# A DLRM tower on one core: both gram rounds at the head of each tile's step, the transposes next to the lookups

## The reference

```
e = stack([tbl_f[ids[:, f]] for f in range(26)], axis=1)          # 2048 x 26 x 128
combined = concatenate([dense[:, None, :], e], axis=1)            # 2048 x 27 x 128
interactions = einsum('bnd,bmd->bnm', combined, combined)
z = concatenate([dense, interactions[:, triu_i, triu_j]], axis=1) # 128 + 351
h = concatenate([z, dense], axis=1)                               # 607
h = maximum(h @ W_top1 + b_top1, 0)                               # 512
h = maximum(h @ W_top2 + b_top2, 0)                               # 256
y = h @ W_top3                                                    # 1
```

## Time and profile before

| | us |
|---|---|
| median of 3 timed runs | 425.25 |
| lowest and highest | 422.16, 428.37 |
| span of the profiled execution | 631.9 |
| TensorE matmul busy in it | 404.1 |
| GpSimd busy in it | 281.3 |
| VectorE busy in it | 222.2 |
| ScalarE busy in it | 198.5 |

### The profile page before, as it was taken

One profiled execution on the slowest core, in us unless ns is written; L12 is line 12 of the kernel. 1 busy time (PEld: TensorE's weight loads), 2 busy tenths in 40 slices (PEclk: granted clock), 3 DMA queues, 4 the chain that ended last, 5 costly groups with the idle time before them and its releaser, 6 DMA issues.

```text
span 631.9 us, 14126 instructions
## 1 busy us (share of the span) xinstructions
PE 404.1 (64%) x6097; PEld 357.1 (57%) x6097; DVE 222.2 (35%) x216; ACT 198.5 (31%) x286; POOL 281.3 (45%) x293
## 2 busy tenths in 40 slices
PE   2620774625966487842887568674486946968677
PEld 2610663624856375832777556574475835858566
DVE  4631454514533152412334144140351414534221
ACT  2410223222434142420244214232041421435523
POOL 6777427372535437360272625546046362630000
PEclk9775678777878679875697758896579866879878
DMA  5642102212111122012020121111212012110010
GB/s 133 189 154 55 35 23 57 79 51 78 38 36 38 45 75 56 23 46 75 15 56 22 47 82 35 48 29 47 64 26 56 26 46 77 38 32 32 28 56 1
DMA packets 22371, 33.91 MB, mean 54 GB/s; under 512 B 8300, under 2 KB 15036, under 8 KB 22310
## 3 DMA queue, kind: packets, MB, share of 16 engines
q0 software_dynamic: 9248, 18.93, 11.6%
q1 hardware_dynamic: 13062, 14.04, 6.8%
HBM read 29.30 MB, written 3.68 MB: 52 GB/s over the span
## 4 chain that ended last, share of the span: by engine, by line
PE 53%; issue 24%; another core or an unknown queue 11%; ACT 5%; DMA 3%; DVE 2%; SPq 1%; ACTq 0%; DVEq 0%
PE hot_ps L566 21%; PE gram_ps L590 12%; PE transpose_ps L543 4%; PE mlp_ps L613 4%; PE mlp_ps L603 3%; PE mlp_ps L601 3%; PE mlp_ps L602 3%; DMA embed_t<-table 3%; ACT embed_t L385 2%; PE hot_ids_ps L548 1%; DVE one_hot L460 1%; ACT embed_t L348 1%; ACT hidden_hi L360 1%; DVE table_lo L464 0%
## 5 line engine op out<-in xcount | busy, mean ns | idle before, releaser
L322 POOL DMA_INDIRECT rows<-table,ids_sb x288 | 280.4, 974 | 277.2 <-PE transpose_ps L543 176.5
L566 PE MATMUL hot_ps<-one_hot,table_hi 125*128 125x256 f32 x512 | 170.7, 354 | 71.4 <-ACT embed_t L385 53.5
L460 DVE TENSOR_TENSOR one_hot<-hot_ids_ps,row_numbers_sb 125x1024 fp32r<-125x1024 f32 x128 | 156.2, 1233 | 129.1 <-remote 68.1
L566 PEld LDWEIGHTS hot_ps<-one_hot,table_hi 125*128 125x128 f32 x512 | 122.2, 239 | 79.4 <-issue 38.6
L566 PE MATMUL hot_ps<-one_hot,table_lo 125*128 125x256 f32 x512 | 158.2, 330 | 3.5 <-issue 3.5
L590 PE MATMUL gram_ps<-embed_t 128*27 128x27 f32 x4096 | 79.8, 213 | 118.5 <-issue 113.9
L590 PEld LDWEIGHTS gram_ps<-embed_t 128*27 128x27 f32 x4096 | 63.1, 125 | 137.7 <-issue 133.3
L566 PEld LDWEIGHTS hot_ps<-one_hot,table_lo 125*128 125x128 f32 x512 | 123.2, 241 | 4.3 <-issue 4.3
L348 ACT COPY embed_t<-transpose_ps 128x512 f32<-128x512 f32 (+1 forms) x80 | 92.8, 1160 | 81.0 <-remote 43.0
L446 DVE COPY_PREDICATED units<-late_sb,gram_ps 128x208 f32<-128x208 int32 x32 | 34.8, 1089 | 159.8 <-ACT units L379 159.6
L385 ACT COPY embed_t<-hot_ps 128x256 f32<-128x256 f32 x64 | 44.4, 694 | 81.0 <-PE hot_ps L566 41.5
(11 more groups left out here) (40 smaller groups left out, 242.7 us busy)
## 6 DMA issues: line engine op xcount, KB each, us to landing
rows<-table,ids_sb POOLq DMA_INDIRECT x288
embed_t<-table SPq DMA_DIRECT2D x8, 500.0 KB
bounce<-units SPq DMA_DIRECT2D x8, 448.0 KB, 2.5
scratch<-bounce SPq DMA_DIRECT2D x7, 378.0 KB
rows<-dense SPq DMA_DIRECT2D x16, 64.0 KB
scratch<-w SPq DMA_DIRECT2D x1, 512.0 KB
scratch<-w_units SPq DMA_DIRECT2D x2, 252.0 KB
rows<-bounce SPq DMA_DIRECT2D x1, 378.0 KB
```

The lines of the kernel that those rows point to most:

```text
L322: nc.gpsimd.indirect_dma_start(rows[:, t2, f, :], None, tables[table], bass.IndirectOffsetOnAxis(ids_sb[:, slot, table:table + 1], 0)).the ...
L460: nc.vector.tensor_tensor(one_hot[:, half], ids_over, numbers_over, ALU.is_equal).then_inc(one_hot_ready, 1)
L566: last = nc.tensor.matmul(hot_ps[:, 0:GROUP], table[:, k, step, :], one_hot[:, half, j, :], start=(step == 0 and table is table_hi), stop= ...
```

## The change

In both lists of `STEPS` G1 comes right behind G0, at the head of the step. The five transpose banks follow, each behind one lookup, and the MLP stages come later in the first step (M2 after M1; Q4 ahead of M0) and stay between lookups in the second. Since the last round of a group is now done early in the second step, its pack may reach its landing while the MLP of the group before still uses `scratch`; SP therefore waits, between the store and the landing, for the copy of M6 of the group before (`MLP_USES` is 7). The last group's landing is elsewhere and has no such wait.

```diff
 STEPS = [
-    "B0 G0 H0 H1 Q0 G1 H2 Q1 H3 S0 Q2 H4 Q3 H5 W0 M0 H6 W1 M1 Q4 M2 H7 W2 M3".split(),
-    "G0 H8 M4 H9 Q0 M5 H10 Q1 H11 M6 H12 Q2 H13 W3 Q3 H14 W4 Q4 H15 G1".split(),
+    "B0 G0 G1 H0 Q0 H1 Q1 H2 Q2 H3 Q3 S0 H4 Q4 H5 W0 M0 H6 W1 M1 M2 H7 W2 M3".split(),
+    "G0 G1 H8 Q0 M4 H9 Q1 M5 H10 Q2 H11 Q3 M6 H12 Q4 H13 W3 H14 W4 H15".split(),
 ]
@@
                 sp.dma_start(bounce, units[:, buf].rearrange("p k q -> p (k q)")).then_inc(units_stored, 16)
                 sp.wait_ge(units_stored, 16 * (g + 1))
 
+                if landing is packed_raw:
+                    sp.wait_ge(mlp_copied, MLP_USES * g + 1)
                 by_row = bounce.rearrange("(s n) x -> s (n x)", s=BLOCK)[:, 0:N * UNITS * GROUP_BLOCKS]
```

## The result

The changed kernel takes 457.5 us (455.6 to 458.3, 4 runs), the kernel before 425.2 (422.2 to 428.4, 4 runs): 1.075 times as long, 95% interval 1.070 to 1.081. I forecast 423. (Single executions over 1.5% above the fastest of their kernel stay in the medians given here; the ratios leave them out.)

What follows compares the result with a forecast made beforehand. The prediction took GpSimd's gathers to bound the kernel (407 to 423 us): 10.4 us of new TensorE waits vanish in 48 us of slack, and the earlier pack brings 2, so 425.25 - 2 = 423 us, range 411 to 436.

Steps and rivals of the forecast that it cites:

- The breaks: TensorE's issue waits in the gram rounds, taken as a recording cost: 152 and 70 us out of 631.9 leave 410.
- the slack of 6.9 us a group: TensorE's steady group of 39.0 us against 45.9 us for the gathers, so TensorE has 6.9 us to spare.
- Who leads: GpSimd's gathers held likelier to bound the kernel, 407 to 423 us, than TensorE, 402 us without steady waits.
- rival A: Whole kernel: TensorE leads and the new waits count in full, 425.25 + 10.4 - 4.8 = 431 us; chance 0.15.
- G1 beside G0: Gram rounds: PSUM reuse costs 0; G0, now right behind H15, waits for H15's copy, 0.74 us a group.
- Banks and lookups: Lookups waiting for copies: 0.70 plus 0.74 us a group against 0.70 before; with G0's wait 10.4 us in all.
- Pack earlier: Pack of a group's last round starts a step earlier: nothing in steady groups, up to 4.8 us gained at the end, 2 credited.
- The wait on SP: SP's landing of a pack waits for M6 of the group before: cost 0, with 11 us before it is needed.
- Moved work: Work shifted between steps: TensorE 2.5 us late at each odd tile, then catching up; GpSimd a tile ahead, not stopped.
- B: TensorE leads and its clock falls after one longer wait for a tile's gathers: 444 us in full, 435 partly; chance 0.15.
- C: The pack is late in steady groups too, so starting it earlier gains 9.7 us: 416 us; chance 0.20.
- D: Whole kernel: the order isn't felt at all, since the gathers lead to the very end: 425 us; chance 0.15.

Runs made afterwards that it cites:

- e5b: The kernel before with each gram round cut into two halves set apart, plus 64 tiny matmuls ahead of all TensorE steps: 411.8 us, ratio 0.977.
- e3: The kernel before with G1 later in the first step and behind H12 in the second, so no two rounds are neighbours: 440.95 us, ratio 1.038.
- e1: The kernel before with only G1 moved behind G0 in both steps and SP's wait added, banks left in place: 441.0 us, ratio 1.038.

## Why the prediction was wrong, step by step

**The breaks.** The step that failed is the first: "I take the breaks to be a cost of recording". The arithmetic that seemed to bear it out, 631.9 less 152 and 70 is 410, mixed a fact of another chip with one of the kernel. The evidence against it stood in the view: the earlier trace rows put 113.9 us of issue waits into the gram rounds, and no row gave recording a reason to pick these. With the breaks real, TensorE's group is not 39.0 us but 47.6, and the slack of 6.9 us a group isn't there. Of the 8.6 us, the rounds have 4.3 (11.1 for 6.8, the jumps back among them), lookups and broadcasts 3.2 (19.3 for 16.1), transposes 0.9 (5.15 for 4.2).

**Who leads.** The gathers' side was right to the microsecond. The last gather should start at 3.3 + 367 less one, 369 us, and does so in before (369.78) and in e5b (369.02). But in before another 54 us follow, not 37: TensorE trails by some 17 us, so it leads the time, as in rival A. "TensorE needs 23 us of losses that I don't see": they were the breaks that I had crossed out, 19.8 us, and the clock behind them.

**G1 beside G0.** Costed at 0 for the reuse of PSUM and 0.74 a group for the bare copy ahead of G0. The second is there (2.9 us at G0 in four places, 0.7 in one before). The term of 0 is where most of the loss went: the edit made a second pair of rounds in each group. B0, rounds and H15 grew by 3.4 us a group, 20 us in groups 1 to 6; a part of this is position, as the shifts show.

**Banks and lookups.** Waits of lookups behind copies went from 7.4 to 13.2 us, those of G0 from 0.7 to 2.9: 8.0 us for a forecast of 10.4. Right in size, and, since TensorE leads, not hidden. The other figure that I gave for bunched banks, 17 us, is not borne out: the lookups' part is 5.8 us. The Trainium skill (TensorE: Matmul & The Clock Gate, the table ahead of its first part) has the first-in first-out queue from which I had worked it out; the price is what was wrong here.

**Pack earlier.** Forecast: nothing in steady groups, up to 4.8 at the end, 2 credited. From the first gram matmul of group 7 on the kernel needs 46.1 us for 51.3, 5.2 gained; in the second profile of the changed kernel (`e8_after`) 48.6, 2.7 gained. But the wait for the lower half didn't get shorter, 1.54 us for 1.14, so "no wait for the lower half" was wrong: the landing was issued at 404.92, and the cast that reads it ran only at 416.79, behind ScalarE's other work. What got shorter are the last group's rounds, 8.6 us for 12.7 (9.5 in `e8_after`): breaks again, in code that the change leaves alone. Whether a later pack would have made these shorter rounds wait isn't shown, and so the 2 us aren't either. The waits, before and after:

```profile
384.76 0.38 PE L601 MATMUL mlp_ps<-packed_hi,w1u_hi 126*128 126x256 f32 x1 [1.14 <-DVE packed_lo L464]
```

```profile
418.72 0.39 PE L603 MATMUL mlp_ps<-packed_hi,w1u_hi 126*128 126x256 f32 x1 [1.54 <-DVE packed_lo L466]
```

**The wait on SP.** Cost 0, and no engine is seen waiting for it. SP's and ScalarE's timeline of the changed kernel:

```profile
130.69 0.33 SPq L248 DMA_DIRECT2D bounce<-units  x1
...
139.08 0.35 SPq L254 DMA_DIRECT2D scratch<-bounce  x1
...
161.92 0.92 ACT L375 CAST packed_hi<-scratch 126x768 fp32r<-126x768 f32 x1
```

The landing goes out 8.4 us after the store, and the cast that reads it comes 22.8 us later.

**Moved work.** "GpSimd works a tile ahead, so nothing stops it" was wrong for this kernel as it ran: GpSimd waited 28.3 us for transposes, up to 8.5 at a time, and its last gather came 21.8 us late. It was an effect and no cause: half a piece of shift brings the wait to 2.1 us with the same order.

**The rivals.** B named the right side and two right parts (TensorE leads, its clock falls), 435 to 444 us, for another reason. It had TensorE wait for a tile's last gathers; the changed kernel waits for a bank's copy ahead of a round once in the whole run, 1.4 us. The clock fell behind the breaks. A was right that TensorE leads and that the waits count in full. C's steady wait for the pack isn't there: the kernel before waits for the lower half only twice, 1.7 us in all, both in what follows group 6. D is excluded.

**What stays open.** Why e3, with no rounds side by side, is as slow as e1: its position wasn't varied, and neither was the pack whose transfers run beside its late packet. When a code packet starts is not understood: 1.1 us after a resume in the pairs (200.81 and 201.93), 8.6 us after the last packet in e3. Open, too, is why one chip takes 1.5 times as long for the same kernels, and ranks the halved rounds last. There the gram matmuls come in handfuls, as in the first profile of before, in its timeline of TensorE:

```profile
285.96 0.28 PE L590 MATMUL gram_ps<-embed_t 128*27 128x27 f32 x3 [1.22 <-issue]
287.37 0.20 PE L590 MATMUL gram_ps<-embed_t 128*27 128x27 f32 x1 [1.13 <-issue]
```

A slower supply of code would look like this; no run measured it by itself.

## What to carry to other kernels

Count instructions, not only work: where 256 of an engine's instructions run in less than about 3.5 us, the next ones come late. So cost two such runs side by side as more than the sum of both, and try runs of half the length with wide matmuls between them: here halved rounds set apart won 15 us, while whole rounds set further apart lost 15. Before an edit of the order is judged by a few per cent, shift the whole instruction stream by half a piece and by a whole one; here that alone moved one kernel by 12 us and the other by 27. And if the span of a profile is far from the median, take the same kernel's profile again before explaining the difference away.

## What the runs showed of the hardware

- **In runs of tiny matmuls TensorE's code comes in pieces of 256 instructions, and the next is usable 3.46 to 3.73 us after the last.** Seen as breaks of mostly 1 to 2.7 us labelled "issue" that end 2.2 to 2.5 us after a 16 KB packet has started; where a packet started late, the break was 3.1 us (`e3_spread`). The Trainium skill (Runtime: NRT & Kernel Launch, Instruction fetch mechanics) has the same 16 KiB and 256 instructions, and says that crossing into the next block is mostly hidden. The block size agrees with these traces; that it is hidden doesn't, for matmuls that start every 13.5 ns (126 in 1.70 us).
- **A jump back of the hardware loop cost 2.1 to 4.8 us**, twice in each kernel: 4.7 and 4.4 in before, 4.2 and 4.0 after the change (193.77 in the chain above), 2.7 and 2.1 in the changed kernel with half a piece of shift.
- **More columns made a kernel faster**: 27 to 54 columns, with the count of instructions unchanged, took some 10 us off; the granted clock was 0.946 for 0.896, and the lookups of a group took 20.6 us for 21.8.
- **Chips differ**: 425 and 642 us for one and the same kernel, timed.
